# Opening the ternary feedforward inside the long convolution of a six-stage decoder kernel

## What is computed

```python
def _L1_xattn_ref(k, v, q, ssm_kernel, D, head_dim):     # k = v = context, q = x
    kv = jnp.einsum('bhil,bhjl->bijhl', k_, v_)
    y = jnp.fft.irfft(rfft(kv, n) * rfft(ssm_kernel, n), n)[..., :L]   # long convolution over the channel axis
    out = y + kv * D
    out = jnp.einsum('bijhl,bhil->bjhl', out, q_)
def _L1_ffn_ref(x, w1, b1, ln_g, ln_b, w2, b2):
    h = jax.nn.silu(bitlinear158(x, w1, b1))              # 512 -> 2048
    h = jax.nn.gelu(h, approximate=False)
    h = layer_norm(h, ln_g, ln_b)
    return bitlinear158(h, w2, b2)                        # 2048 -> 512
def bitlinear158(x, w, b):
    xq = act_quant(rms_norm(x))     # 127 / max|.| per row, rounded
    wq = weight_quant(w)            # -1, 0, 1 times one scale
    return xq @ wq.T + b
```

## Time and profile before

| | us |
|---|---|
| median of 3 runs | 2049.9 (2035.58 to 2051.96) |
| the profiled execution's own time | 2051.19 |
| its span | 2049.4 |
| TensorE busy | 1782.9 (87%) |
| VectorE busy | 1429.8 (70%) |
| ScalarE busy | 996.2 (49%) |
| GpSimd busy | 507.6 (25%) |
| convolution block, first to last instruction | 1592.3 to 1786.1 |
| ternary block | 1786.9 to 2044.3, and its last store |

### The profile page before, as it was taken

How to read it: one execution, slowest core, us unless ns; L and a number is a source line. 1 busy time by engine, 2 the same in 40 slices (tenths; PEclk the granted TensorE clock), 3 DMA queues, 4 the chain that set the end, 5 groups by cost and what they waited for, 6 DMA issues and landing times. The chain is left out here.

```text
span 2049.4 us, 33014 instructions
## 1 busy us (share of the span) xinstructions
PE 1782.9 (87%) x12284; PEld 1370.8 (67%) x12302; DVE 1429.8 (70%) x2847; ACT 996.2 (49%) x1680; POOL 507.6 (25%) x531
## 2 busy tenths in 40 slices
PE   4489999687769999999999997999998799668886
PEld 2255665324459999999999986777885577534443
DVE  8478888587935666566566564666666589639997
ACT  3436666624424444444444443333443244469995
POOL 5133331152110100000000021001100499724322
PEclk9679999857979999999999998999999899869998
DMA  6499886322512122222221324222222544120001
GB/s 164 45 101 98 96 95 70 117 85 89 175 40 59 55 79 70 65 75 60 71 78 58 117 65 141 81 86 70 94 73 78 119 103 98 50 95 11 18 25 31
DMA packets 148482, 163.92 MB, mean 80 GB/s; under 512 B 46240, under 2 KB 100384, under 8 KB 146528
## 3 DMA queue, kind: packets, MB, share of 16 engines
q1 hardware_dynamic: 143076, 151.85, 32.7%
q10 hardware_dynamic: 5248, 9.96, 1.3%
HBM read 116.86 MB, written 19.48 MB: 67 GB/s over the span
## 5 line engine op out<-in xcount | busy, mean ns | idle before, releaser
L1661 ACT ACTIVATE f_gate<-f_gu 128x256 f32<-128x256 f32 x264 | 98.8, 383 | 269.7 <-PE f_gu L1525 190.1
L1802 DVE TENSOR_TENSOR f_hid<-f_gate,f_gu 128x256 f32<-128x256 f32 x264 | 108.4, 421 | 157.5 <-ACT f_gate L1661 153.4
L570 DVE TENSOR_REDUCE a_rowmax<-a_ring 128x2 f32<-128x512 f32 x256 | 165.1, 688 | 52.6 <-PE a_ring L652 50.4
L2675 PE MATMUL e_py<-e_kv,e_toep 128*128 128x288 f32 x640 | 163.3, 412 | 15.6 <-DVE e_kv L2702 15.3
L523 ACT ACTIVATE a_prob<-a_sT 128x1024 f32<-128x1024 f32 x128 | 130.8, 1028 | 48.9 <-PE a_sT L641 48.9
L2675 PEld LDWEIGHTS e_py<-e_kv,e_toep 128*128 128x128 f32 x640 | 120.9, 193 | 47.9 <-DMA e_toep<-lags 15.7
L1538 PE MATMUL f_gu<-f_lowh,f_bg 128*128 128x256 f32 x704 | 141.5, 283 | 5.2 <-POOL f_lowl L1443 5.0
L1525 PE MATMUL f_gu<-f_xhi,f_wg 128*128 128x256 f32 x704 | 131.3, 284 | 0.0
L1525 PE MATMUL f_gu<-f_xhi,f_wu 128*128 128x256 f32 x704 | 130.5, 283 | 0.0
L1807 DVE TENSOR_TENSOR f_hl<-f_hid,f_hh 128x768 fp32r<-128x768 f32 (+2 forms) x90 | 84.5, 939 | 56.0 <-ACT f_hh L1709 54.9
L1538 PEld LDWEIGHTS f_gu<-f_lowh,f_bg 128*128 128x128 f32 x704 | 115.9, 191 | 9.8 <-POOL f_lowl L1443 5.3
(11 more groups left out here) (435 smaller groups left out, 4870.0 us busy)
## 6 DMA issues: line engine op xcount, KB each, us to landing
f_entry<-in_WdT SPq DMA_DIRECT2D x89, 256.0 KB, 2.8
d_staging<-in_w SPq DMA_DIRECT2D x16, 1024.0 KB, 5.7
a_qs<-a_hi SPq DMA_DIRECT2D x64, 128.0 KB, 7.2
a_ks<-a_hi SPq DMA_DIRECT2D x64, 128.0 KB, 6.1
e_toep<-lags SPq DMA_DIRECT2D x16, 512.0 KB, 3.8
f_entry<-in_Bg SPq DMA_DIRECT2D x89, 64.0 KB, 1.9
f_entry<-in_Bu SPq DMA_DIRECT2D x89, 64.0 KB, 2.0
cf<-in_xT SPq DMA_DIRECT2D x4, 1024.0 KB, 7.7
```

Of the source, the lines that this page charges most:

```text
L570: dve.tensor_reduce(rowmax[:, s % 2, :, e * SLOTS + j], ring[n % RING][:, :].rearrange("p (q t) -> p q t", t=T), AX.X, ALU.max, negate=Tru ...
L1661: act.activation(gate[:, i % 2, :], gu[n % 3][:, 0, :], ACT.Silu).then_inc(s_["gate_ready"], 1)
L1802: dve.tensor_tensor(hid[:, j, :], gate[:, i % 2, :], gu[n % 3][:, 1, :], ALU.mult).then_inc(s_["hid_ready"], 1)
L2675: last = pe.matmul(py[n % RING][:, 0:YS], toep[:, u, h % 2, (t - j) * P:(t - j + 1) * P], kv[:, h % 2, j, :, :].rearrange("p b c -> p (b c ...
```

## The change

The convolution's block opens the feedforward. `ternary_early` allocates what both blocks share; `p1` now lies in the four PSUM banks of the convolution's ring. The bias row, weights, gain, shift and b2 are loaded by SP between the convolution's own loads (iterations 4 to 14). ScalarE squares tiles 0 to 11 (one per iteration, n = 3 to 14) and rounds the bias row; VectorE makes the constants, the bias split in two halves (n = 2, 3), the peaks of tiles 0 to 3 (n = 4 to 7), the scales of group 0 (n = 9) and the quantised tile 0 (n = 10); GpSimd makes the roots of group 0 (n = 8); TensorE turns scales and tile 0 through `px` (n = 10, 11), and after the last weighed head makes tile 0's 20 products. `turn_x(0)` is moved ahead of `convolve(0)`. In the ternary block ScalarE begins with the Silu of tile 0.

```diff
+def group_scales(dve, xs, g, wmean, of, fore_ready, lift_ready):   # the nine instructions as before
+def ternary_products(pe, g, t):                                    # the 4 + 16 products as before
 def long_convolution(nc, io, sem, keep):
+        py = [g["p1"][:, n * 512:(n + 1) * 512] for n in range(RING)]
   sync:
                 contexts(0)
+                sp.dma_start(brow[:, :], io["b1"].broadcast_to([4, INNER])).then_inc(s_["b1_in"], 16)
                 for n in range(NT):
                     taps(n)
                     tokens(n)
+                    if 4 <= n < 4 + 2 * KT + 3:
+                        ternary_load(n - 4)
   gpsimd, between sums(2n) and sums(2n + 1), behind root(n - 2):
+                    if n == 8:
+                        pool.wait_ge(s_["t_ssq"], GT)
+                        ... meansq of 4 tiles, then xroot of 4 tiles
   scalar, at the head of iteration n:
+                    if n == 11:
+                        act.wait_ge(s_["t_turned"], 1)
+                        act.activation(g["lrows"][:, 0, :], px[0:4, :], ACT.Copy).then_inc(s_["t_read"], 1)
+                    if n == 12:
+                        act.wait_ge(s_["t_turned"], 2)
+                        act.activation(g["q1f"][:, 0, :, :], px[:, :]..., ACT.Identity, bias=g["minus"][:, :]).then_inc(s_["t_read"], 1)
   scalar, at the end of iteration n:
+                    if 3 <= n < 3 + 3 * GT:
+                        q = n - 3
+                        act.activation(g["junk_x"][:, q % GT, :], rows[:, q, :], ACT.Square, accum_out=g["ssq"][:, q:q + 1])
+                    if n == 1:
+                        act.activation(bhigh[:, :], brow[:, :], ACT.Copy).then_inc(s_["t_bhigh"], 1)
   tensor:
                 def turn_x(n):
+                    if n in (12, 13):
+                        pe.wait_ge(s_["t_read"], n - 11)
+                turn_x(0)
                 for n in range(NT):
                     convolve(2 * n)
-                    if n == 0:
-                        turn_x(0)
                     if n + 1 < NT:
                         turn_x(n + 1)
                     convolve(2 * n + 1)
                     if n >= 1:
                         turn_z(n - 1)
+                    if n == 10: ... 4 transposes of lcols into px
+                    if n == 11: ... 4 transposes of xq into px
+                pe.wait_ge(s_["z_ready"], SH * KT)
+                pe.wait_ge(s_["t_loaded"], 16 * (2 * KT + 3))
+                pe.wait_ge(s_["t_bpart"], 2)
+                ternary_products(pe, g, 0).then_inc(s_["t_h"], 1)
                 turn_z(NT - 1)
   vector, between weigh(2n) and products(2n + 2):
+                    if 4 <= n < 4 + GT: ... peak of tile n - 4 (128x512)
+                    if n in (2, 3): ... one half of bpart (4x1024)
+                    if n == 9:
+                        dve.wait_ge(s_["t_root"], 1)
+                        group_scales(dve, Chain(dve, s_["t_steps"]), g, wmean, first, s_["t_fore"], s_["t_lift"])
+                    if n == 10: ... xq of tile 0 (128x512)
 def ternary_feedforward(nc, io, sem, keep):
-    STEPS = range(-3, NT + LAST)
+    STEPS = range(NT + LAST)
   sync: the loads are gone
   scalar:
+                silu(0)
+                quantised(1)
+                gelu(0)
                 for s in STEPS:
                     g = group_at(s, 3)
-                    if g is not None:
+                    if g is not None and g == NG - 1:
                         for t in range(g * GT, (g + 1) * GT):
                             act.activation(junk_x[:, t % GT, :], xt[:, t, :], ACT.Square, accum_out=ssq[:, t:t + 1])
   tensor: the products of tile 0 and the turns of tile 0 and group 0 are gone
   vector: constants, scales and peaks of group 0, bpart and xq of tile 0 are gone
```

More of the change, by code:

```diff
@@ L2451, in by_heads, with ternary_early @@
     return ap.rearrange("(b h i) f -> h b i f", b=B, i=2 * SD)[n]
+GT = 4
+def ternary_early(nc, held):
+    fix, g = Maker(nc, held), {}
+    nt = N // P
+    g["w1"] = fix.sb("g_w1", [P, KT, INNER], BF16)
+    g["w2"] = fix.sb("g_w2", [P, IT, D], BF16)
+    g["bpart"] = fix.sb("g_bpart", [4, INNER], F32R)
+    g["gain"], g["shift"] = fix.sb("g_gain", [P, INNER]), fix.sb("g_shift", [P, INNER])
+    g["b2"] = fix.sb("g_b2", [P, D])
+    g["wfac"], g["takes"], g["minus"] = fix.sb("g_wfac", [P, 1]), fix.sb("g_takes", [4, 2]), fix.sb("g_minus", [P, 1])
+    g["xq"] = fix.sb("g_xq", [P, 2, D])
+    g["junk_x"] = fix.sb("g_junk_x", [P, GT, D], BF16)
+    g["q1f"] = fix.sb("g_q1f", [P, 2, KT, P], BF16)
+    for name in ("ssq", "peak", "meansq", "xroot", "top", "back1", "fore1", "inv1", "lift"):
+        g[name] = fix.sb(f"g_{name}", [P, nt])
+    g["lhigh"] = fix.sb("g_lhigh", [P, nt], F32R)
+    g["lcols"] = fix.sb("g_lcols", [P, nt, 4])
+    g["lrows"] = fix.sb("g_lrows", [4, 2, GT * P], F32R)
+    g["p1"] = fix.ps("g_p1", [P, INNER])
+    return g
@@ new lines, in ternary_products @@
+def ternary_products(pe, g, t):
+    for n in range(INNER // 512):
+        pe.matmul(g["p1"][:, n * 512:(n + 1) * 512], g["lrows"][:, t // GT % 2, t % GT * P:(t % GT + 1) * P],
+                  g["bpart"][:, n * 512:(n + 1) * 512], start=True, stop=False)
+    for n in range(INNER // 512):
+        for j in range(KT):
+            last = pe.matmul(g["p1"][:, n * 512:(n + 1) * 512], g["q1f"][:, t % 2, j, :], g["w1"][:, j, n * 512:(n + 1) * 512],
+                             start=False, stop=(j == KT - 1))
+    return last
@@ L2753, in ternary_feedforward @@
     NT = N // P
-    GT = 4
     NG = NT // GT
@@ L2757, in ternary_feedforward @@
     LAST = 9
-    STEPS = range(-3, NT + LAST)
+    STEPS = range(NT + LAST)
     own = keep["ternary"]
+    early = own["early"]
+    w2, gain, shift, b2, xq, junk_x, q1f, ssq, peak, meansq, xroot, back1, fore1, lcols, lrows, minus, p1 = (early[n] for n in (
+        "w2", "gain", "shift", "b2", "xq", "junk_x", "q1f", "ssq", "peak", "meansq", "xroot", "back1", "fore1", "lcols", "lrows",
+        "minus", "p1"))
     wmean, winv = own["wmean"], own["winv"]
@@ L2831, in _ @@
             def _(sp):
[L2832 to L2840, removed]
                 for t in range(NT):
@@ L2918, in _ @@
                     t = tile_at(s, 0)
[L2919 to L2924, removed]
+                    if t is not None and t >= 2:
+                        quantised(t)
                     t = tile_at(s, 6)
```

209 lines of the change are left out of this document (110 added, 99 removed).

## The result

The changed kernel takes 2029.59 us (median of 15 runs, 2026.82 to 2034.9), the kernel before 2040.55 beside it (15 runs, 2034.6 to 2051.96). The ratio is 0.9938 with the interval [0.9919, 0.9958]: faster by 8.6 to 16.5 us, which is more than its measurement is uncertain and less than 1%. The forecast was 9.3 less than before. Its time, 2040.6, was 11.0 too high.

The account below looks back on a forecast made before the run. TensorE was taken to bound the convolution, VectorE and ScalarE the middle of the ternary stage, a serial chain its head. Convolution +11.9 and ternary -21.2 gave -9.3, so 2040.6 us, range 2028 to 2047.

Parts of the forecast that it names:

- The ternary block, -21.2,: Head of the ternary block: products of tile 1 start 18.7 us earlier, group 2's squares leave the waits, about 2.5 more.
- the upper bound of 23: Ternary block: largest gain, 23 us, if TensorE's clock falls better in the first tiles.
- The convolution, +11.9,: Convolution block: 0.3 + 0.9 - 0.5 + 6.4 + 2.7 + 1.1 + 1.0 us longer from the inserted work.
- the stall of 6.4: Convolution, n = 9: scales on VectorE wait for GpSimd, an insertion of 9.1 less 2.7 slack stalls TensorE 6.4 us.
- The clock behind it: Convolution after the n = 9 stall: TensorE at half speed for 5.3 us loses 2.7 us, 0 if the clock holds.
- bpart: Convolution, VectorE's bias halves: 1.2 us and a wait of about 1.2 each, costing +1.1 us (0 to 3).
- xq and turn_x(12) behind `t_read`: Convolution, xq at n = 10 and TensorE's turn waiting for ScalarE's `lrows`: +1.0 us (0 to 4).
- The start: Convolution's start: turn_x(0) first delays convolve(0) by 2.2 us, a later stall goes; result +0.3 (-1.7 to +5.8).
- The end: Convolution's end: tile 0's 20 products hidden in TensorE's idle time, last turn made warm, -0.5 us; +2 if cold.
- No lock: Rival, chance 0.24: small VectorE operations slip past GpSimd, convolution costs 0.7, the change gives -20.5, 2029.4 us.
- Late rows: Rival, chance 0.12: the first rows land late and convolve(0) waits, +5.5 on the forecast, 2046.1 us.
- The clock stays low: Rival, chance 0.04: after the n = 9 stall TensorE stays at 1.2 GHz; three such iterations give 2067.6 us.

Follow-up runs that it names:

- two experiments: Against the changed kernel (2030.56): sums of heads 17 and 18 replaced by memsets, 2021.64 us; intermediates of the n = 9 scales put in PSUM, 2024.51 us.
- the second profile of the changed kernel: The changed kernel measured again, nothing edited, beside the kernel before (2048.02 us): 2030.56 us, ratio 0.9924.

## Why the prediction came out as it did

**The difference** was forecast at -9.3 and measured at -12.6 (by the ratio), inside the forecast's own terms, and within 1% as it held likeliest. All runs together give 14.0 to 16.0, and the profiles say as much: convolution and ternary stages together take 457.1, 454.2 and 457.1 before, 440.3 and 440.0 after, so 14 to 17 less. In the first pair the forecast was short by 7.5: 5.1 in the convolution (+6.8 for +11.9) and 2.4 in the ternary block (-23.6 for -21.2).

**The time**, 2040.6, is 10.7 over the 2029.9 of all 21 runs: 4.0 by the base (2049.9 of three runs for 2045.9 of 94) and 6.7 by the difference (9.3 for 16.0). The spread of the base was in sight: three runs from 2035.58 to 2051.96.

**The ternary block, -21.2,** held. The products of tile 1 begin 18.87 earlier in relation to the block (forecast 18.7), the squares of group 2 are out of the chain of waits (Silu 3 gains 2.5 over Silu 2). In the end it gave 23.6 and 23.3 against the profiles that missed the high clock in the first tiles and 20.2 to 20.5 against the one that met it; the upper bound of 23 named that cause and is passed by 0.6 in the first case: Silu 2 follows Silu 1 by 7.74 in the changed kernel and by 9.36 in the profiles that missed it. The clause that group 1's squares "give nothing" was true of the old head, where ScalarE made them from 12.2 to 14.7 after the block's start and still waited 5.21 for the products behind them, and is false of the new one: with the head gone, they are worth 8. It did no harm to the sum, since they were taken out along with it.
The drain behind a table load that the Trainium skill states (ScalarE: Activation LUTs, "What ACT_TABLE_LOAD costs") isn't seen: Silu 0 begins 0.02 after its load ends, Gelu 0 likewise, and Gelu 0's load begins 0.02 after the operation ahead of it.

**The convolution, +11.9,** was the step that failed, by size: measured +6.8 (201.47 against 194.66). Its largest term, the stall of 6.4, measured 4.4. The mechanism was right and two experiments show it, from the side of GpSimd and from the side of the operand. What was mis-sized:

- The nine scales: 6.62 for 9.1. I let one operation pass in each gap of GpSimd's; in fact a short one often gets in ahead of the one that waits (0.22 and then 1.17, 0.17 and then 0.70), and the scales were over before the three small root operations came. The stall is then 4.4 (1711.35 + 0.44 to 1716.15) for 6.4, close to 6.62 and the 0.24 behind them, less the slack of 2.7, which held.
- The clock behind it: 1.9 for 2.7 (2.8 in two other profiles).
- bpart: no stall, for +1.1. The halves took 1.26 and 1.82.
- xq and turn_x(12) behind `t_read`: no stall, for +1.0.
- The start: 0.3 to 1.6 from the order over the eight profiles that have it, for 0.3; 1.6 in this one. The first turn waited until 11.7 after the block's first transfer (1604.46), where I had put the rows at 1602, and until 10.3 to 10.9 in the others. In the profile of the changed kernel the first products then met more of the high clock (6.09 for 7.84), which hid it. The second convolve of this pair begins only 0.06 later in the block; only the table above shows the two parts.
- Two sets of four transposes, +0.9: as forecast.
- The end: the products of tile 0 are hidden and the last turn is warm (0.66 for 1.12), as forecast, but only 0.1 of the 0.5 arrives: from the last convolve to the ternary block it takes 12.14 for 12.28.

The sum of the mechanisms is 1.6 + 0.9 - 0.1 + 4.4 + 1.9 = +8.7 (8.56 unrounded), less 1.75 of luck with the first 20 products: the 6.8 measured.

**The rivals.** "No lock" gave 2029.4, which is the measured median, and it is wrong: the wait for GpSimd is there and costs 6 to 7. Its time was hit by luck: its difference of -20.5 is 4.5 too large against the 16.0 of all runs, and the base was 4.0 too high. "Late rows" is true in kind, at 0.3 to 1.6 us where it had 5.8. "The clock stays low" didn't happen: it was back at 0.96 in the window from 1720, 4 us after the restart.
The rule of the Trainium skill (SBUF — State Buffer, "SBUF: two separate sides") is borne out as far as these rows go: the two-input operations wait too (2.20 and 0.70), as does the tensor-scalar (1.15) and the cast (1.17). The rows of before had shown only the tensor-scalar. Of the nine, three have two inputs in SBUF (L2481, L2486, L2492), and not four as the prediction counted. The four peaks, with one input, didn't wait, as the prediction said by that rule. They took 0.67 to 0.68 beside GpSimd, and where the two overlap whole neither is longer, here VectorE and GpSimd at n = 6:

```profile
1675.26 0.68 DVE L2862 TENSOR_REDUCE g_peak<-x_rows 128x1 f32<-128x512 f32 x1
```

```profile
1675.26 0.73 POOL L2639 TENSOR_TENSOR e_zf<-e_planes 128x256 f32<-128x256 f32 x1
```

So "all operands in SBUF" is not by itself what makes a VectorE operation wait; the kind of operation counts too.

## What to carry to other kernels

Before work is inserted beside a busy GpSimd, look where the operands of the VectorE operations lie: nine operations worth 1.5 us cost 6.6 with all operands in SBUF, and 1.5 again with one in PSUM (the reciprocal and the peaks didn't mind). Take the base from as many runs as its spread asks for, and compare profiles from the first instruction that the change can touch, since 9.5 us came from stages it never touches. What gives nothing beside a wait can cost more than its own time once the wait is gone: the squares of group 1 are 2.5 us of ScalarE and cost 8.0.

## What the runs showed of the hardware

The collision works in both directions. In the changed kernel VectorE and then GpSimd, at n = 3:

```profile
1643.52 1.82 DVE L2867 SCALAR_TENSOR_TENSOR g_bpart<-g_bhigh,g_takes,g_brow 4x1024 fp32r<-4x1024 f32 x1
```

```profile
1644.64 2.93 POOL L2635 TENSOR_TENSOR e_planes<-e_planes 128x1024 f32<-128x1024 f32 x1 [0.36 <-ACT e_planes L2701]
```

The VectorE operation began 0.02 before a GpSimd operation of 0.74 (1643.54 to 1644.28) and took 0.56 more than its twin of n = 2 (1.26), which ran almost wholly in a pause of GpSimd (1632.97 to 1634.06). GpSimd's next began 0.70 before that one's end (1645.34) and took 0.57 more than usual (2.36). In the second profile of the changed kernel the two took 1.80 and 2.91. The reciprocal of 128x4, at 0.17 across the end of one GpSimd operation and the start of the next (1709.05), waited for neither.
